# Routing inside the second attention: where the vector engine makes its two expert choices, and where ScalarE makes their exponentials

## What is computed

```python
q = (hidden_states @ Wq).reshape(B, S, H, dh)      # B = 8, S = 512, H = 16, dh = 64
k = (hidden_states @ Wk).reshape(B, S, H, dh)
v = (hidden_states @ Wv).reshape(B, S, H, dh)
scores = jnp.einsum('bqhd,bkhd->bhqk', q, k) * scale + position_bias
probs = jax.nn.softmax(scores, axis=-1)
ctx = jnp.einsum('bhqk,bkhd->bqhd', probs, v).reshape(B, S, H * dh)
attn_output = ctx @ Wo
...
logits = xf @ w_router                             # 1024 tokens by 8 experts
probs = jax.nn.softmax(logits, axis=-1)
gate, eidx = jax.lax.top_k(probs, K)               # K = 2
gate = gate / jnp.sum(gate, axis=-1, keepdims=True)
oh = jax.nn.one_hot(eidx, E, dtype=jnp.float32)
pos = jnp.cumsum(oh.reshape(N * K, E), axis=0) - 1.0
```

## Time and profile before

| | us |
|---|---|
| median of three runs | 1545.58 |
| lowest, highest | 1542.42, 1548.46 |
| the profiled execution, its own time | 1540.97 |
| its span, first to last instruction | 1539.2 |
| second attention in it, up to its last steps | some 550 to 1412 |

### The profile page before, as it was taken

The page is one execution under the profiler, slowest core; times in us unless marked ns, Lnnn a source line. Parts: engine busy times, 40 slices in busy tenths (PEclk is TensorE's granted clock), DMA queues, the critical chain, the costliest instruction groups (busy, mean ns, idle before and its releaser), DMA issues. The chain is left out here.

```text
span 1539.2 us, 22455 instructions
## 1 busy us (share of the span) xinstructions
PE 1262.3 (82%) x6711; PEld 636.3 (41%) x6711; DVE 934.0 (61%) x2823; ACT 871.7 (57%) x1716; POOL 511.0 (33%) x787
## 2 busy tenths in 40 slices
PE   3887787878736669999999998999998999998193
PEld 1333332332214424454454454454544544544162
DVE  5445455444220147878879879778798798784210
ACT  1887676667512246756666656666576576662041
POOL 2002211222142613323343442433443443434245
PEclk7999998788557879999999999999999999998597
DMA  6275663357208626657557656656676575565062
GB/s 167 85 188 125 160 162 116 67 138 162 34 7 258 179 55 160 156 123 169 139 142 158 158 137 146 165 130 153 150 158 145 131 160 141 118 148 142 25 149 26
DMA packets 138040, 205.25 MB, mean 133 GB/s; under 512 B 35406, under 2 KB 80413, under 8 KB 137920
## 3 DMA queue, kind: packets, MB, share of 16 engines
q1 hardware_dynamic: 109952, 146.01, 37.3%
q0 software_dynamic: 27392, 56.76, 17.3%
q10 hardware_dynamic: 576, 1.05, 0.2%
HBM read 61.75 MB, written 46.58 MB: 70 GB/s over the span
## 5 line engine op out<-in xcount | busy, mean ns | idle before, releaser
L1487 ACT ACTIVATE tile<-tile,low 128x512 f32<-128x512 f32 x512 | 363.7, 714 | 265.6 <-DVE low L1574 259.9
L1268 POOL DMA_DIRECT2D crossed<-blocks x512 | 253.6, 506 | 505.4 <-DVE blocks L1587 484.1
L1574 DVE CUSTOM_DVE_ANT_0 tile<-s_ps,bias 128x512 f32<-128x512 f32 x512 | 330.5, 682 | 46.8 <-PE s_ps L1351 37.9
L599 ACT ACTIVATE probs_a<-score_ps,gbound 128x1024 f32<-128x1024 f32 x256 | 269.2, 1113 | 134.9 <-PE score_ps L845 110.9
L1351 PE MATMUL s_ps<-kT,qT 64*128 64x512 f32 x1024 | 267.9, 631 | 23.8 <-DVE low L1574 16.0
L1587 DVE STREAM_TRANSPOSE blocks<-tile 128x512 f32<-128x512 f32 x384 | 256.6, 694 | 0.0
L1371 PE MATMUL o_psb<-crossed,v_b 128*64 128x512 f32 x512 | 237.0, 606 | 9.7 <-DMA crossed<-blocks 9.7
L859 PE MATMUL o_ps<-probs_a,v_ext 128*32 128x512 f32 x1024 | 157.1, 691 | 0.8 <-issue 0.8
L336 POOL DMA_INDIRECT slots<-rows_r,slot_r x128 | 127.8, 998 | 88.0 <-issue 53.2
L845 PE MATMUL score_ps<-q_stack,k_stack 32*128 32x512 f32 x512 | 103.6, 558 | 53.4 <-ACT probs_a L599 34.3
L1351 PEld LDWEIGHTS s_ps<-kT,qT 64*128 64x128 f32 x1024 | 85.7, 187 | 139.5 <-issue 91.4
(11 more groups left out here) (159 smaller groups left out, 1625.0 us busy)
## 6 DMA issues: line engine op xcount, KB each, us to landing
crossed<-blocks SPq DMA_DIRECT2D x512, 96.0 KB
crossed<-blocks POOLq DMA_DIRECT2D x512, 96.0 KB
inv_row<-inv_rows SPq DMA_DIRECT2D x128, 128.0 KB
q_parts<-parts SPq DMA_DIRECT2D x32, 256.0 KB, 3.9
k_stack<-k_parts SPq DMA_DIRECT2D x32, 256.0 KB, 3.7
q_stack<-q_parts SPq DMA_DIRECT2D x32, 256.0 KB, 4.8
bias_skew<-bias_rows SPq DMA_DIRECT2D x8, 1024.0 KB
w_f<-in_w SPq DMA_DIRECT2D x32, 256.0 KB, 5.4
```

The costliest lines, as they stand in the source:

```text
L599: nc.scalar.activation(probs[q % 2][:, c % 4 // 2, pair:pair + 2, :].rearrange("p h t -> p (h t)"), score_ps[c % 2][:, :], ACT.Exp, bias=g ...
L1268: pool.dma_start(strip_to(n, a, m), strip_from(n, a, m)).then_inc(crossed_sw[n % 2], 16)
L1487: nc.scalar.activation(tile[(b * NS + k) % RING][s][:, :], tile[(b * NS + k) % RING][s][:, :], ACT.Exp, bias=low[n % 2][:, s, i:i + 1], sc ...
L1574: nc.vector.tensor_tensor_reduce(out=tile[(b * NS + k) % RING][s][:, :], in0=s_ps[k % 2][s][:, :], in1=bias[:, h, off:off + S], scale=1.0, ...
```

## The change

The exponential of the router moves on ACT from the end of step 10 to its beginning. The first choice moves on DVE from the end of step 11 to the end of step 10, behind the normalized rows of the next batch. The second choice moves from the end of step 11 to the end of step 12, ahead of the counts. No instruction is added or dropped, and the lists of PE, POOL and SP are the same as before.

```diff
         ROUTE = dict(stats=20, rows=22, turn=(23, 1), copy=23, logits=(25, 1), shift=25,
-                     exps=26, pick=27, runs=28, counts=(29, 1), take=29, address=30)
+                     exps=26, first=26, second=28, runs=28, counts=(29, 1), take=29, address=30)
...
             def step(b, s, more, routed=None):
                 at = laps(b, s, more)
+                if routed is not None and s + ND == ROUTE["exps"]:
+                    r.exps(act, routed)
                 for part in two:
...
-                if routed is not None and s + ND == ROUTE["exps"]:
-                    r.exps(act, routed)
-
...
-                if d == ROUTE["pick"]:
-                    for k in range(TOPK):
-                        r.pick(dve, b, k)
+                if d == ROUTE["first"]:
+                    r.pick(dve, b, 0)
+                if d == ROUTE["second"]:
+                    r.pick(dve, b, 1)
                 if d == ROUTE["runs"]:
                     r.run_counts(dve, b)
                     r.weigh(dve, b)
```

## The result

The changed kernel takes 1530.2 us in the median of six runs (1525.8 to 1535.0), the kernel before 1543.4 in six; the ratio is 0.9913, with a 95% interval of 0.9885 to 0.9942. That is 13 us less (9 to 18). In two further comparisons, on two other chips, which run both kernels some 30 us faster, the same pair gave 0.9895 (0.9856 to 0.9934) and 0.9893 (0.9861 to 0.9924), 16 us less each. The forecast was 10.1 us less, at 1535.5, in a range that ended at 1530.5: right in its sign and in the wait that it named, short in its size. The two times are not 5.3 us apart by the change alone. The forecast started from 1545.58, the median of three runs of the kernel before, and six runs give 1543.4: that is 2.2 us of the 5.3.

The account below looks back on a forecast made before the run. PE sets the pace, with some 35 us idle to win. Three full-cover batches 4.2, three short-cover 3.0, last batch 0.88 and strips 2.0 make 10.1 us: 1545.58 to 1535.5, range 1530.5 to 1544.5.

Parts of the forecast that it names:

- The path: End-of-step-11 choices delay DVE's tile, ACT's copy L1458, then PE in step 13; six waits fall from 11.1 to about 3 us.
- The floor of 1.32 us: In step 13, DVE's tile cannot start sooner than 1.32 us behind the start of its scores on PE.
- The first choice in the cover of step 10: DVE's idle time in step 10 hides the choice, except in three short-cover batches, where PE loses 0.4 us each.
- The second choice: Moved to the end of step 12, step 13's tile comes 1.30 to 1.51 us earlier; taken as 1.4 per batch.
- The last batch: In the last routed batch, PE's 1.08 us wait for DVE's tile falls to 0.20, gaining 0.88 us.
- The strips: Pair 5's transfers for step 14 start about 2.60 us earlier, shortening PE's waits by 2.0 us in all (0 to 3.0).
- The low end: Hand-overs at their worst and strips no better: 7.2 us gained, 1538.4 us; chance 0.20.
- giving back: PE arrives earlier but waits for strips of pairs 4, 6 and 7; 7 to 10 us lost, 1543 to 1546; chance 0.14.
- The pile: At the end of step 12, 2.6 us of DVE work stands before the tile leading to ACT's copy; slower, chance 0.06.
- the slow case: If PE's scores hold DVE's step 12, its end delays tiles 1.09 to 1.30 us per batch; some 1555 us, chance 0.06.
- The port: The first choice blocks POOL's issue of pair 4's transfers; up to 5.3 us lost, 1540.8 us; chance 0.03.
- The strict reading of the busiest-engine rule: Reordering VectorE while TensorE's list stays the same gains nothing, 1545.6 us; counted with given back, chance 0.14.

Follow-up runs that it names:

- The pad of step 12: Changed kernel plus three idle reductions, some 1.5 us together, on DVE at the end of step 12 in seven batches; ratio 0.9986 to the kernel before.
- the moved piece of v: Changed kernel with PE's and ACT's last piece of v moved from step 9 to step 11 in batches 1 to 7; ratio 0.9883 to the kernel before.
- step 17: Changed kernel plus three idle reductions on DVE in the middle of step 17 in six batches; ratio 0.9963 to the kernel before.

## Why the prediction fell short

**The path was right.** The waits on L1458 were to fall from 11.1 to 3 or so; they fell to 2.5 in all three profiles. The pad of step 12 shows that they are worth what was claimed. The floor of 1.32 us was reached as well (1.37).

**The first choice in the cover of step 10** was sized at 0.4 in three batches. In the first profile it was 0.13 to 0.16 in five of the six, in the other two 0.09 to 0.16 in four. In the short-cover batches the sum had added full durations. The rows after show that L1600 holds the next instruction off for 0.61 and not for its 0.69, and that the choice starts 0.09 before the end of the rows. The longer cover of the other three batches came from PE's waits for strips in step 10 (1.04, 0.69 and 0.53), which are absent or shorter after the change. Together it cost 0.6 to 0.8 us by this wait and 1.1 by all waits for tiles, where 1.2 was forecast.

**The second choice** was the term that had been worked out most carefully, and on this path it was worth next to nothing by itself. The prediction said so in its sum (2.60 - 1.09 against 1.30) but not in words: of the 1.51, the first choice brings 1.30. What the second choice does bring are the strips of step 14.

**The last batch** was put at 0.88. From its `shifted_r` to the last one it is 3.6, 0.8 and 1.5 us shorter (69.7, 64.9 and 65.6 us before, 66.1, 64.1 and 64.1 after), 2.0 in the mean. Waits of 1.08 and 1.20 there became one of 1.10. Against that, a wait for strips near its end is 3.1 to 3.2 in all three profiles after, and before it is 1.6 in one and absent in two. The time at half clock in this part fell from 24.0, 11.4 and 13.0 us to 12.8, 10.8 and 10.4, which at 1.65 us for each 3.4 is 2.3 us in the mean, as much as the whole gain here. So the 0.88 was not confirmed by itself.

**The strips** were put at 2.0, out of 0 to 3.0, all of it in step 14. There it held: with the last batch these waits fell from 3.3, 3.4 and 2.9 us to 0.9, 1.0 and 0.9, 2.2 in the mean. All waits of PE for strips in batches 1 to 6, whoever the profile names as their end, fell from 6.4, 5.0 and 4.9 us to 2.7, 2.7 and 2.4 in the three pairs, 2.8 in the mean. More than a third of that came in step 10, which the prediction had not named (2.3, 2.1 and 0.4 before, 0.2, 0.7 and 0.9 after). Part of it is luck: a wait of 1.04 and one of 1.03 in step 10 of batch 1, in two of the three profiles before and in no other of the fourteen, end 3.8 us after the first `shifted_r`, before a moved choice has run. They are 0.7 us of the mean.

**The clock was missing from the sum, and this is the step that failed.** "What can be won is its idle time" put the ceiling of the change at the gaps in front of PE's matmuls. In batches 1 to 6 the three profiles of the kernel before have 3.4, 10.2 and 6.8 us at half clock; the three of the changed kernel have none, nor has the one with only the first choice moved, nor the one with the moved piece of v. At half clock a stretch of 3.4 costs some 1.65 us, so this is 3.3 us in the mean. The row that hinted at it was in the profile: the granted clock of 0.99 over the steady part was read as full, though most of what it lacks lies in the last batch. The Trainium skill, page Perfetto Trace Analysis, section Matmul Optimizations, says that the engine "dynamically scales power based on utilization, so it's important that matmuls execute back-to-back in batches". By that rule a wait on PE can cost more than itself, and the trace agrees: where the waits were put back, one of six in step 12 and two of six in step 17 were followed by slow matmuls.

**The sum again,** for batches 1 to 6, means of three profiles each: the waits in front of L1325 (on L1458 and on earlier pieces of v) fell from 13.2 to 4.6 us, those for strips from 5.4 to 2.6, those for tiles rose from 15.8 to 16.9; with the clock's 3.3 that is 8.6 + 2.8 - 1.1 + 3.3 = 13.6. The stretch itself went from 645.0 to 631.1, 13.9. And it closes for each profile by itself: the length of these six batches, less all of PE's waits over 0.1 us, less 0.485 of the time at half clock, is 606.4 to 607.2 us in thirteen of the fourteen profiles (608.3 with the moved piece of v). With the 2.0 of the last batch this is 15.9. By its terms the forecast had 7.2 + 0.9 + 2.0 = 10.1; strips and last batch brought 1.9 more, the net of waits and lateness 0.3, and the clock, which it did not have, 3.3.

**The rivals.** The low end did not happen, and giving back only in the last batch, with its one wait for strips of 3.1. The pile is refuted by the second choice moved alone, and the slow case with it. The port cost nothing. The first choice does run beside POOL's issue in the changed kernel, from 842.46 to 843.80 in batch 2, and the issue takes what it took before, 3.98 us:

```profile
842.18 3.98 POOL L1268 DMA_DIRECT2D crossed<-blocks  x8 [6.95 <-DVE blocks L1586]
```

The choice takes 1.34 us there where it took 1.30, and PE's waits for the strips of pair 4 are 0.33 at most in the three profiles after, 0.44 before. The prediction took this for a case in which the two share a port and one waits; neither waited here. The strict reading of the busiest-engine rule is refuted: PE's list did not change, and PE went through the same part 16.5 us sooner. The range had every listed term at its best in its lower end, 12.1 us, and no room for an unlisted one; in the three pairs of profiles the part from the first to the last `shifted_r` fell by 16.5, 16.2 and 14.9, all beyond these 12.1. The time itself missed the end of the range by 0.3 us, and that is no measure of the error: counted from the 1543.4 of six runs instead of 1545.58, the range would have ended at 1528.3, with 1530.2 inside.

## What to carry to other kernels

When a short side task on one engine sits in front of a tile that a chain of two other engines leads back to the busiest one, look for the nearest idle time of that engine ahead of it and move only what fits: here one choice of 1.3 us fitted, and two did not. Price a wait of the busiest engine at more than its length: test with an idle pad what a wait costs before taking it for the ceiling. Compare stretches between the same two instructions rather than whole spans, when other parts of the kernel vary by more than the change.

## What the runs showed of the hardware that had not been expected

A wait of TensorE of 1.4 to 2.0 us was in some cases, not in most, followed by 3.4 or 6.8 us at 1.2 instead of 2.4 GHz, which started within 1.9 us of the wait's end. All fourteen profiles have 55 such waits in batches 1 to 6, and 13 were followed by it. Of the 32 that are 1.8 us or longer it was 11, of the 23 shorter ones two (one of 1.74 with both choices in step 12, one of 1.47 with both in step 10, where a wait of 1.20 came 2.3 us later). Four of the 55 were waits for strips, of 1.44 to 1.67, and none of them was followed. No stretch at half clock stands in these batches without such a wait ahead of it: the three profiles of the changed kernel and that of the moved piece of v have neither. In the last batch shorter waits did it too. Two of 1.1 to 1.2 us, whose ends lie 2.3 us apart, were followed by it at once in three profiles (twice the kernel before, once both choices in step 12); in other profiles two like them were not. So these runs give no length below which a wait is safe. The Trainium skill, page TensorE: Matmul & The Clock Gate, section HAM oscillation — how this bites in real kernels, has such falls behind waits that recur; here the waits were short, and the falls came behind a minority of them.
